# Merged one-hots for the token sort, and experts' weights copied into a ring, in a spectral filter and mixture-of-experts kernel

## The reference

```python
x = x + conv(ln_c(x))             # 64 -> 16 channels, FFT, gain per bin, inverse FFT, 16 -> 64, residual
t = to_tokens(x)                  # 8192 tokens of 64 numbers
n = ln_t(t)
probs = softmax(n @ gate_w + gate_b)                # 16 experts
top_probs, top_idx = top_k(probs, 2)                # each token goes to two experts
top_probs = top_probs / sum(top_probs)
h = silu(n @ w1[e]) * (n @ w2[e])                   # hidden 128, for the chosen experts e
t = t + sum_over_two(top_probs * (h @ w3[e]))
x = from_tokens(t)
```

## Time and profile before

| | |
|---|---|
| median of 3 runs | 473.91 us (473.31 to 474.52) |
| profiled execution, its own time | 471.76 us |
| its span, first to last instruction | 469.9 us |
| mean granted TensorE clock | 0.798 of full speed |
| PE busy | 384.8 us, 82% |
| DVE, ACT, POOL busy | 231.8, 223.5, 184.7 us |

### The profile page before, as it was taken

One profiled execution on the slowest core, in us unless ns is written; L12 is line 12 of the kernel. 1 busy time (PEld: TensorE's weight loads), 2 busy tenths in 40 slices (PEclk: granted clock), 3 DMA queues, 4 the chain that ended last, 5 costly groups with the idle time before them and its releaser, 6 DMA issues. The chain is left out here.

```text
span 469.9 us, 10372 instructions
## 1 busy us (share of the span) xinstructions
PE 384.8 (82%) x3588; PEld 333.0 (71%) x3588; DVE 231.8 (49%) x572; ACT 223.5 (48%) x420; POOL 184.7 (39%) x157
## 2 busy tenths in 40 slices
PE   5676868658979959879999999978999999777765
PEld 4543568527979758769988877757878787667753
DVE  3958575974283277022222222112566662268864
ACT  5674556503556434334344443424555553266642
POOL 1195013204456417523333310006765400288871
PEclk9859865575699967566698999988999999558765
DMA  8999000001111101401222223242544421233221
GB/s 278 273 350 380 6 1 0 1 0 28 31 40 42 44 7 49 129 15 39 73 70 74 69 73 85 68 99 72 137 103 122 103 69 40 43 85 102 73 68 62
DMA packets 55396, 40.02 MB, mean 85 GB/s; under 512 B 37660, under 2 KB 49692, under 8 KB 54708
## 3 DMA queue, kind: packets, MB, share of 16 engines
q1 hardware_dynamic: 42804, 29.25, 21.5%
q0 software_dynamic: 12384, 10.10, 8.7%
q10 hardware_dynamic: 160, 0.01, 0.0%
HBM read 20.08 MB, written 19.14 MB: 83 GB/s over the span
## 5 line engine op out<-in xcount | busy, mean ns | idle before, releaser
L1297 POOL DMA_INDIRECT xs<-sorted_y,back x64 | 79.1, 1236 | 105.5 <-issue 90.6
L1291 POOL DMA_INDIRECT sorted_x<-xs,addr x64 | 74.2, 1159 | 112.1 <-ACT xs L545 91.6
L1199 DVE SCALAR_TENSOR_TENSOR power<-banks,fold 128x512 f32<-128x512 f32 x46 | 31.8, 692 | 136.1 <-PE banks L876 68.7
L876 PE MATMUL banks<-shared,w_all 128*128 128x128 f16 x368 | 77.5, 241 | 0.1
L875 PE MATMUL banks<-shared,w_all 128*128 128x128 f16 x368 | 75.3, 240 | 0.1
L545 ACT CAST xs<-banks 76x512 f16<-76x512 f32 x64 | 37.2, 582 | 60.3 <-PE banks L801 60.2
L884 PE MATMUL banks<-w_all,power 128*128 x368 | 55.0, 297 | 5.3 <-ACT enh L583 2.1
L884 PEld LDWEIGHTS banks<-w_all,power 128*128 128x128 f32 x368 | 49.1, 207 | 10.8 <-issue 10.8
L801 PE MATMUL banks<-shared,tok 128*76 128x128 f16 x384 | 41.4, 264 | 13.7 <-DVE tok L1149 10.4
L826 PE MATMUL banks<-ident,tok 128*76 128x128 f16 x384 | 43.7, 277 | 5.7 <-DVE tok L1149 5.2
L1149 DVE TENSOR_SCALAR tok<-perm,local 128x304 f16<-128x304 f16 x144 | 36.7, 303 | 22.1 <-PE banks L826 19.5
(11 more groups left out here) (176 smaller groups left out, 593.1 us busy)
## 6 DMA issues: line engine op xcount, KB each, us to landing
sorted_x<-zeros SPq DMA_DIRECT2D x2, 2944.0 KB, 30.8
w_raw<-sorted_x SPq DMA_DIRECT2D x22, 256.0 KB, 2.9
sorted_y<-filt SPq DMA_DIRECT2D x96, 32.0 KB
sorted_y<-enh SPq DMA_DIRECT2D x88, 32.0 KB
w_raw<-in_L_ffn_w SPq DMA_DIRECT2D x5, 512.0 KB, 15.4
xs<-in_x SPq DMA_DIRECT2D x8, 256.0 KB, 4.1
out<-cen_sq SPq DMA_DIRECT2D x8, 256.0 KB, 3.6
shared<-in_t_fwd SPq DMA_DIRECT2D x1, 1024.0 KB, 7.5
```

The source lines that it names most:

```text
L876: last = nc.tensor.matmul(dst, of_expert(experts[(i % 2) * QUAD + b], a + 1, HID).bitcast(F16), tokens[:, b, :, :], start=False, stop=True)
L1199: nc.vector.scalar_tensor_tensor(hid[:, q % RING, :], bank[2 + q % 2], HSCALE / WSCALE, gated[:, q % 2, :], ALU.mult, ALU.mult).then_inc(h ...
L1291: nc.gpsimd.indirect_dma_start(out=sorted_x[k].rearrange("(g s) c -> g (s c)", s=GRP), out_offset=bass.IndirectOffsetOnAxis(ap=addr[:, k, ...
L1297: nc.gpsimd.indirect_dma_start(out=yl[m % YL_RING], out_offset=None, in_=sorted_y[k].rearrange("(g s) c -> g (s c)", s=GRP), in_offset=bas ...
```

## The change

There are two parts.

**The sort.** `one_hots` writes one matrix for both choices: the second choice's one-hot first, then one instruction that adds the first choice's onto it, with a wait between them (`hot_second`). A tile's rows get three more columns (`rows`, `ROW = 131`): the second choice's weight in high and low halves, and the number of the first expert. `sort_tile` is then four matmuls of 131 columns, and there are no matmuls of two columns. Their result goes to one place in PSUM for both halves (`SORT_PAIR`, a pair of banks), and ScalarE copies it out in two instructions, the rows and the three columns (`wcol`). `turn_hots` is four transposes with f16 results. Which choice a slot belongs to is found afterwards: `experts_of_groups` gives the expert of each group, and `slot_weights` takes the second weight, or `WT_SCALE` less it where the group's expert is the token's first. The ring of one-hots has 6 places. `weights(0)` stands before `sort_places(0)`.

**The weights.** VectorE loads the owners into its registers and copies the 640 16-bit numbers a partition of each block's expert from `w_all` to a ring of four quads (`fetch`, two quads ahead, `FETCH_AHEAD = 2`). TensorE reads the ring at fixed addresses (`weights_of`) and waits for `fetched`. The eight additions of the mean move from VectorE to GpSimd, between the last scatter and the first gather.

The core of the diff:

```diff
-HOTS = 4
+HOTS = 6
-SORT_PAIR = (6, 7)
-HOTT_BANK, WLOC_BANK, Y_BANK, XT_BANK = 3, 5, 4, 6
+ROW = 2 * C + 3
+ROW_STRIDE = 2 * C + 4
+MISC_BANK, SORT_PAIR, HOTT_BANKS, Y_BANK, XT_BANK = 3, 2, (6, 7), 6, 7
...
-                nc.scalar.copy(sorted_t[n % SORT_RING], bank[SORT_PAIR[n % 2] if n < HT else SORT_PAIR[1]][0:TGROUPS, :]).then_inc(sorted_done, 1)
+                sorted_rows = banks[SORT_PAIR][0:TGROUPS, :, 0:2 * ROW_STRIDE].rearrange("g a (b n) -> g a b n", b=2)
+                nc.scalar.copy(sorted_t[n % SORT_RING].rearrange("g (a b n) -> g a b n", a=2, b=2), sorted_rows[:, :, :, 0:2 * C]).then_inc(sorted_done, 1)
+                nc.scalar.copy(wcol[:, n // HT, n % HT, :, :].rearrange("g (a b) n -> g a b n", a=2), sorted_rows[:, :, :, 2 * C:ROW]).then_inc(wcol_done, 1)
...
             def sort_tile(n):
                 k, t = n // HT, n % HT
                 pe.wait_ge(hot_done, n + 1)
...
                 if t == 0:
                     pe.wait_ge(wt_done, k + 1)
-                    if k:
-                        pe.wait_ge(wloc_done, k)
+                if n >= 1:
+                    pe.wait_ge(wcol_done, n)
                 for s in range(GRP):
-                    at = 2 * (GRP * t + s)
-                    for j in range(2):
-                        last = nc.tensor.matmul(bank[WLOC_BANK][0:TGROUPS, at:at + 2], hots[n % HOTS][:, j, :, s], wt_parts[:, k, j, t, :],
-                                                start=(j == 0), stop=(j == 1))
-                last.then_inc(wloc_ps, 1)
+                    at = (s % 2) * ROW_STRIDE
+                    last = nc.tensor.matmul(banks[SORT_PAIR][0:TGROUPS, s // 2, at:at + ROW], hots[n % HOTS][:, :, s], rows[:, n, 0:ROW], start=True, stop=True)
+                last.then_inc(sort_ps, 1)
...
-                    for j in range(2):
-                        last = nc.tensor.matmul(dst[:, s * P:(s + 1) * P], hots[use % HOTS][:, j, :, s], ident16[:, :], start=(j == 0), stop=(j == 1))
+                    last = nc.tensor.transpose(dst[0:TGROUPS, s * P:(s + 1) * P], hots[use % HOTS][:, :, s], ident16[:, :])
...
-            def of_expert(e, a, width):
-
-                return w_all[:, bass.ds(e, 1), a * HID:a * HID + width].rearrange("p o n -> p (o n)")
-
-            def up(k, i, experts):
+            def weights_of(q, b, a, width):
+
+                return fetched_w[:, (q % RING) * QUAD + b, a * HID:a * HID + width]
+
+            def up(k, i):
                 q, n = NQ * k + i, OCTETS * k + i // 2
                 if i % 2 == 0:
                     pe.wait_ge(xt_done, n + 1)
+                pe.wait_ge(fetched, q + 1)
...
-                for j in range(2):
-                    last = nc.vector.tensor_scalar(hots[use % HOTS][:, j, :, :].rearrange("p g s -> p (g s)"), slot_iota, local[:, k, j, t:t + 1],
-                                                   None, ALU.is_equal)
-                last.then_inc(hot_done, 1)
+                hot = hots[use % HOTS].rearrange("p g s -> p (g s)")
+                nc.vector.tensor_scalar(hot, slot_iota, local[:, k, 1, t:t + 1], None, ALU.is_equal).then_inc(hot_second, 1)
+                dve.wait_ge(hot_second, use + 1)
+                nc.vector.scalar_tensor_tensor(hot, slot_iota, local[:, k, 0, t:t + 1], hot, ALU.is_equal, ALU.add).then_inc(hot_done, 1)
+
+            def experts_of_groups(k):
+
+                nc.vector.tensor_reduce(group_expert[:, k, :], stepped.rearrange("p (e t) -> p t e", e=E), AX_X, ALU.add)
...
+            def fetch(q):
+                k, i = q // NQ, q % NQ
+                n, o = OCTETS * k + i // 2, i // 2
+                if i % 2 == 0:
+                    used = regs[n % 2][0:blocks_of(o)]
+                    nc.vector.load(used, owner[0:1, k, o * OCT:o * OCT + len(used)])
+                    experts[n] = [nc.vector.snap(r, min_val=0, max_val=E - 1) for r in used]
+                if q >= RING:
+                    dve.wait_ge(y_ps, q - RING + 1)
+                for b in range(QUAD):
+                    last = nc.vector.tensor_copy(fetched_w[:, (q % RING) * QUAD + b, :],
+                                                 w_all[:, bass.ds(experts[n][(i % 2) * QUAD + b], 1), :].rearrange("p o n -> p (o n)"))
+                last.then_inc(fetched, 1)
...
                     product(q)
+                    if q + FETCH_AHEAD < HALVES * NQ:
+                        fetch(q + FETCH_AHEAD)
                     if k == 0:
                         for n in sorts_in(i):
                             one_hots(n)
```

More of the change, by code:

```diff
@@ L82 @@
 DOWN_LAG = 2
+FETCH_AHEAD = 2
 RING = 4
@@ L786, in owners_for @@
                 pe.wait_ge(past_done, k + 1)
-                nc.tensor.matmul(bank[4][0:HT, 2 * P:2 * P + SLOT_BLOCKS], ones[0:E, 0:HT], past[:, k, :], start=True, stop=True).then_inc(owner_ps, 1)
+                nc.tensor.matmul(bank[MISC_BANK][0:HT, 2 * P:2 * P + SLOT_BLOCKS], ones[0:E, 0:HT], past[:, k, :], start=True, stop=True).then_inc(owner_ps, 1)
             def sort_tile(n):
@@ L1095, in route @@
                 step(first_of(chosen[:, k, 0, :, :], lg, m1))
+                step(nc.vector.tensor_scalar(rows[:, HT * k:HT * (k + 1), ROW - 1], top[:, k, :], -1.0, float(E), ALU.mult, ALU.add))
                 step(nc.vector.scalar_tensor_tensor(lg2[:, k, :, :], chosen[:, k, 0, :, :], -FAR, lg[:, k, :, :], ALU.mult, ALU.add))
@@ L1105, in weights @@
                 step(nc.vector.tensor_tensor(wt[:, k, 1, :], wt[:, k, 0, :], ratio[:, k, :], ALU.mult))
-                step(nc.vector.tensor_copy(wt_parts[:, k, :, :, 0], wt[:, k, :, :]))
-                nc.vector.tensor_tensor(wt_parts[:, k, :, :, 1], wt[:, k, :, :], wt_parts[:, k, :, :, 0], ALU.subtract).then_inc(wt_done, 1)
+                high_at, low_at = (rows[:, HT * k:HT * (k + 1), 2 * C + a] for a in range(2))
+                step(nc.vector.tensor_copy(high_at, wt[:, k, 1, :]))
+                nc.vector.tensor_tensor(low_at, wt[:, k, 1, :], high_at, ALU.subtract).then_inc(wt_done, 1)
             def rounded_up(out, in_f, count, offset, scale, unit):
@@ L1173, in _ @@
             route(0)
+            weights(0)
             sort_places(0)
@@ L1177, in _ @@
                     logits_out(1)
-                    weights(0)
+                if t == 2:
+                    experts_of_groups(0)
                 if t == OWNERS_AFTER + HOTS:
@@ L1185, in _ @@
                     owners_of(1)
+                    experts_of_groups(1)
                 one_hots(t)
             weights(1)
-            for n in range(NBLK):
-                add_mean(n)
             slot_weights(0)
@@ L1192, in _ @@
                 one_hots(HT + n)
+            regs = [[nc.vector.alloc_register(f"owner{s}_{b}") for b in range(OCT)] for s in range(2)]
+            experts = {}
+            def fetch(q):
[11 more added lines that the diff above has]
+                last.then_inc(fetched, 1)
             def product(q):
@@ L1231, in return_end @@
                 add_tiles((HT * (k + 1)) // TURN - 1)
-            dve.wait_ge(x1t_done, NBLK)
+            dve.wait_ge(wsplit, 3)
+            dve.wait_ge(owner_done, HALVES)
+            for q in range(FETCH_AHEAD):
+                fetch(q)
             for k in range(HALVES):
@@ L1306, in _ @@
                 scatter(n)
+            pool.wait_ge(mean1_done, 1)
+            for n in range(NBLK):
+                pool.wait_ge(tok_done, n + 1)
+                nc.gpsimd.tensor_tensor(ct_cen[:, 4 * n:4 * n + 4, :, :], ct_cen[:, 4 * n:4 * n + 4, :, :],
+                                        per_tile(mean1[:, BT * n:BT * (n + 1)], C), ALU.add).then_inc(x1t_done, 1)
             for m in range(HALVES * HT):
```

116 lines of the change are left out of this document (51 added, 65 removed).

## The result

The changed kernel takes 482.4 us (median of 4 runs, 481.4 to 483.7); the kernel before, run beside it, takes 474.2. The ratio is 1.017, with a 95% interval from 1.014 to 1.021: slower by 1.7%, where 456 us were forecast. The time lies just past the upper end of the range, 482 us. The profiled execution took 481.35 us with a span of 479.3 us. In every ratio executions more than 1.5% above the fastest of their kernel are left out.

The account below looks back on a forecast made before the run. TensorE, or a ring of waits through it, was taken to set the pace until about 400, GpSimd in the last 65 us. Terms summed to -18.1 from 471.8, so 453.7; median forecast 456 us, range 434 to 482.

Parts of the forecast that it names:

- 12 quads with sort: Quads carrying the sort of half 1: 6.5 us each instead of 6.18, so +4, from -5 to +9.
- 10 bare quads: Quads with neither sort nor return: 2.4 us instead of 3.35 once the clock is up; -8, from -10 to +2.
- 16 return quads: Quads that also return half 0: 3.9 us each against a period of 3.75; +3, from -3 to +10.
- the sum of 6.9 at the lower clock: Sort quad: matmuls, product, copies, one-hot, sorts and ScalarE added up to 6.9 us at TensorE's lower clock, 5.8 at full.
- the clock that stays low: Rival: TensorE's clock stays low behind new VectorE waits; +0.7 in each of 12 sort quads, +22, 496 us; chance 0.08.
- VectorE replaces TensorE as the bound: Return quads: VectorE's 2.42 us a quad gets 1.24 more, 3.66 against a period of 3.75, so the gain is gone.
- 10 us there are hidden: Between the halves: the mean's eight additions on GpSimd, idle until its first gather, cost nothing; without that cover, 10 us.
- this rival to the gathers: Rival: copies and GpSimd's indirect DMAs hold each other up, two gathers a return quad; +36, some 490 us; chance 0.10.
- the price of a copy: VectorE's weight copies of 128 x 640 16-bit numbers: four elements a cycle, 0.26 us each taken, four 1.04.
- the step of 1.5 us a tile: Sort of half 0, 32 tiles: 1.5 us a tile instead of 2.07, saving 18.2 us; net -16.5.
- everything overlaps: Rival: the clock stays up, with sort quads 5.8 and return quads 3.6 us; sum -38, 436 us; chance 0.13.
- one element a cycle: Rival: slower weight copies on VectorE, +2.0 us on some 45 quads, about 530 us; chance 0.03.

Follow-up runs that it names:

- Run 7: Changed kernel with copies behind the one-hots and return steps, but in half 0 the wait for the down matmuls still right behind the product: 0.967 of the kernel before.
- run 1: Changed kernel with its sort part alone: TensorE again addresses the experts' weights through its own registers and VectorE copies none; 0.963 of the kernel before.
- run 5: Changed kernel with every weight copy made twice, the extra four a quad to a place that nobody reads: 1.082 of the kernel before.
- run 4: Changed kernel with the eight mean additions back on VectorE, ahead of the weights of half 0's slots: 0.998 of the kernel before.
- run 3: Changed kernel with each quad's copies moved last, behind the one-hots (half 0) and the return steps (half 1): 451.3 us, 0.934 of the kernel before.
- run 6: Changed kernel with fillers, matmuls that nobody reads, in TensorE's idle time ahead of the sorts in the 12 sort quads: 0.994 of the kernel before.

## Why the prediction was wrong, point by point

| term | forecast | measured |
|---|---|---|
| places and sort of half 0, until its last turn | -15.4 | -10.1 |
| all up to the first product | -16.1 | -10.9 |
| 12 quads with sort | +4 | +17.0 |
| 10 bare quads | -8 | -2.2 |
| 16 return quads | +3 | +16.9 |
| other quads of half 1 | -3 | -6.5 |
| tail and end | +2 | -4.0 |

With the gap between the halves (-0.8) the right column from the second row on adds up, but for rounding, to the +9.4 by which the span grew. Against the forecast -18.1 the miss is 27.5 us: the sort quads make 13.0 of it, the return quads 13.9, the bare quads 5.8 and the time up to the first product 5.2, less what the last rows give back.

*12 quads with sort: the failed step is the sum of 6.9 at the lower clock, and the 6.5 taken.* The sum had the copies at 1.24 ahead of the one-hot, which is right, but not the wait that the copies bring with them: 8.7 us in the 12 quads, 0.73 a quad. With it the sum is 7.6, and 7.60 was measured; that the two meet so exactly is in part luck, as the single quads lie between 6.8 and 8.4. Run 7 prices the wait at 0.55 and the copies at 1.08. The forecast then lay between the clocks; the granted clock went down to 0.59. It named that danger and priced it at 0.7 a quad; the fillers measured 0.8. This rival, the clock that stays low, did come in these quads. It had the new VectorE waits as its cause, and run 1 shows 0.59 without the copies, so fewer sort matmuls go with the lower clock as well; by itself it cost next to nothing there (6.28 us), as the gain of the sort paid for it.

*16 return quads: the failed step is "VectorE replaces TensorE as the bound", 3.66 us of work against a period of 3.75.* That takes idle time for free time. In the earlier trace rows VectorE was idle 1.3 us a quad, 21.2 in all: 12.6 for a silu that stood on ScalarE behind the high part of VectorE's own weighing, and 8.4 for TensorE. Work put ahead of the weighing moves the silu back by its whole length: 0.92 for 1.03 us of copies once the ring is closed (run 5). The first four copies cost 1.05; as five quads still waited for TensorE before, and the owner registers are loaded too, that 1.05 and 1.03 agree is in part chance. Behind the weighing about half of it fits into that time: 3.93 to 4.47 in the nine runs with this order, for 3.75.

*10 bare quads: the failed step is "10 us there are hidden" for the mean additions.* GpSimd had the time, but its order put the additions behind the last scatter, on top of VectorE's copies. The Trainium skill, SBUF - State Buffer, Who interferes with whom, says that a VectorE copy in a two-port mode and a GpSimd instruction shut each other out for a whole instruction. This trace agrees for the additions, and shows more: the copy of 6.5 us stood through some six additions of 1.03 us each (none was above 0.67 without them, run 4). Beside the indirect DMAs no copy waited for a whole instruction of 1.13 us, and of the 64 gathers (median 1.134 us) the longest took 1.375, 0.24 more, about one copy. Other runs have single gathers of up to 4.96 us, but the kernel before has one of 4.27 without any copy. The forecast applied this rival to the gathers, where it did not hold, and did not ask it of the additions that it moved itself. Without them a quad took 2.54 and 2.23 to the 2.4 forecast.

*Sort of half 0: the tile was right (1.5 forecast, 1.47 measured), what lies around it was not.* TensorE waited 3.63 us for the owners instead of 1.2, because with six buffers VectorE works through ten one-hots first, and the places of half 1 took 12.3 us (150.25 to 162.52) instead of 10.0. Together 4.7 of the 5.3 us that were missing. The first logits also came 1.6 us later (86.57 for 85.00), in code that the change leaves alone. That is 6.3 in all, so 1.0 us was won somewhere else; where, stays open.

*Right were:* the price of a copy, the removal of the register instructions (56 ns apart), the step of 1.5 us a tile, and the small copy (0.17 us long). The tail was expected to lose 2 us; its gathers ran at 38.95 / 32 = 1.22 us against 1.33 before, and it gained 4.0. The other quads of half 1 gained 6.5 instead of 3. Both made the miss smaller.

*Two sums of the rivals are off.* The terms of "everything overlaps" add up to -40 and not -38, so 434 us, which is where the range begins. For one element a cycle, 2.0 us on 45 quads is 90, so some 546 us by its own terms and not 530. Neither touches the forecast.

## What to carry to other kernels

Idle time of an engine is free only if its next wait does not depend on the work that you would delay; before adding work, follow the wait that ends the idle time back, and if it comes round to the same engine, put the work behind the instruction that others wait for. Here that order was worth more than either part of the change. Price a new instruction together with the waits it must carry. When two engines' work is moved onto each other's time, ask of each moved instruction what it shares with the other.

## What the runs showed of the hardware

- A VectorE copy of 128 x 640 16-bit numbers takes 0.319 us and 0.24 between starts, but one that met eight GpSimd additions (128 x 512, f32) took 6.5 us, and 5.9 in run 3; beside GpSimd's indirect DMAs none of 184 took over 0.67 (run 4).
- Matmuls whose weights are addressed through a register start 120 ns apart and more behind the first few of a quad; at a fixed address they start 56 ns apart at full clock.
- Taking matmuls from a stage can cost what they took: in run 1 TensorE was busy 9 us less in the sort quads, the granted clock was 0.59 instead of 0.82, and the stage was as long as before. In the changed kernel matmuls that nobody reads, put into TensorE's idle time, brought 0.59 to 0.82 (run 6).
